# Two position-wise front layers: image-major tokens, rings of three and no hardware loops

## The chip, the core and the metric

The kernel runs on one core of one Trainium2 chip, in one launch. The metric is the device time in microseconds. Before the change it is 6516.77 us, the median of 3 runs (6513.06 to 6520.01). The core has a matrix engine (TensorE, PE in the profile), a vector engine (VectorE, DVE), an activation engine (ScalarE, ACT), a general engine (GpSimd, POOL), and a queue engine (SyncE, SP) that issues most of the DMAs.

## The reference, cut to what matters

The input is 64 images of 32 x 32 positions with 32 channels in float32. Six residual layers follow each other. Only the first two change here:

```
x = x + L0(_gn(x))   # per position (l,h): gelu(x @ W1[l,h] + b1[l,h]) @ W2[l,h] + b2[l,h]
x = x + L1(_gn(x))   # expanded = x @ W_exp.T + b_exp, split in primary and gating (32 + 32)
                     # s = 0.9*s + 0.1*gating along the 32 image rows, s0 = 0
                     # out = (primary * sigmoid(s)) @ W_con.T + b_con
_gn: per image and channel, (v - mean) / sqrt(var + 1e-5) over the 1024 positions
```

After them come a squared-score attention layer, an expert-choice layer, and one block with softmax attention and a router. They read the two layers' output from DRAM as rows `t1` of 32 channels a position, and they make up the larger part of the time.

## The kernel before, in words

`positionwise_layers` does both front layers in one block. Four neighbouring positions of an image row lie with their 32 channels on the 128 partitions, so an image is 256 columns; eight columns are one image row. The tile `xt` holds all 64 images, `[128, 256 columns, 64 images]`: the image is innermost. One chunk is one image row of all images, 8 x 64 = 512 elements a partition; there are 32 chunks a layer (`ROWS`). All engines walk the chunks in hardware loops of two chunks a turn (`pairs`), with two buffers of everything.

- `statistics(n)`, L197 to L219: 64 `bn_stats` of VectorE (L199), one an image, each reading 256 elements that lie 64 words apart. Two small matmuls with `share` (L387) average over the four partition groups, and GpSimd takes the power of minus one half (L168). It runs once ahead of each layer.
- Layer 0. VectorE subtracts the mean (L234), scales (L236), adds the first bias (L244), adds the second bias (L250), and adds to `xt` (L254). TensorE multiplies with the weights of each position, `products` at L397: 8 columns x 4 groups of 32 partitions, each a 32x32 float32 product over 64 images that the trace shows as two matmuls with a weight load each, so 64 matmuls for the first product and 64 for the second. ScalarE does one GELU a chunk (L343). SyncE loads a chunk's two weight tiles (L135, L136) into one of two buffers, once the second product of the chunk two before it is done (`out_made`).
- Layer 1. Three matmuls 128x512 a chunk (L431 main, L432 gate, L436 contraction), each two in the trace. ScalarE scales the gate product by 0.1 (L357), VectorE does the running average `0.9*ema + drive` (L281), ScalarE takes the sigmoid (L362), VectorE gates (L288) and adds to `xt` (L293).
- Rows out. For each image and half, GpSimd copies 128 columns into `staged` (L173), TensorE transposes them (L459), VectorE copies them out of PSUM (L319) and SyncE stores an image (L142).

The order within an engine is the order of its program; semaphores link the engines. The next layer's block begins when all engines have come to the end of this one.

Of the kernel before, what the change touches and what calls it, by code (L numbers as in the profile page):

```python
# [6 lines left out]
F32 = mybir.dt.float32  # L7
BF16 = mybir.dt.bfloat16
ACT = mybir.ActivationFunctionType
# [14 lines left out]
def pairs(eng, lo, hi, body):  # L24

    turns = (hi - lo) // 2
    with eng.Fori(0, turns) as k:
        for u in range(2):
            body(2 * k + (lo + u), (lo + u) % 2)
    if (hi - lo) % 2:  # L30
        body(hi - 1, (hi - 1) % 2)


def positionwise_layers(nc, t):
# [3 lines left out]
    with ExitStack() as ctx:  # L38
        def sb(name, shape, dt=F32):
            return ctx.enter_context(nc.sbuf_tensor(name, shape, dt))  # L40

        def ps(name, shape, dt=F32):
            return ctx.enter_context(nc.psum_tensor(name, shape, dt))

        def sem(name):
            return ctx.enter_context(nc.semaphore(name))

        xt = sb("xt", [P, NI, B])
# [11 lines left out]
        w1 = sb("w1", [P, 2, NC, C])  # L60
        w2 = sb("w2", [P, 2, NC, C])
        xn = sb("xn", [P, 2, CH])
        xc = sb("xc", [P, 2, CH])
        pre = sb("pre", [P, 2, CH])
        hid = sb("hid", [P, 2, CH])
        res = sb("res", [P, 2, CH])
# [5 lines left out]
        b_gate10 = sb("b_gate10", [P, 1])  # L72
        b_con = sb("b_con", [P, 1])
        drive = sb("drive", [P, 2, CH])
        ema = sb("ema", [P, 2, CH])
        gate = sb("gate", [P, 2, CH])
        gated = sb("gated", [P, 2, CH])
        staged = sb("staged", [P, 2, P])
        rows = sb("rows", [P, 2, 2, P])

        p_hid = [ps(f"p_hid{u}", [P, CH]) for u in range(2)]
        p_out = [ps(f"p_out{u}", [P, CH]) for u in range(2)]
        p_gate = [ps(f"p_gate{u}", [P, CH]) for u in range(2)]
        p_rows = [ps(f"p_rows{u}", [P, CH]) for u in range(2)]
        p_stat = p_gate[0]
        p_main, p_con = p_hid, p_out

        loaded = sem("loaded")
        small_loaded = sem("small_loaded")
        zeroed = sem("zeroed")  # L90
        consts = sem("consts")
        w_in = [sem(f"w_in{u}") for u in range(2)]
        chain = sem("chain")
        moment_ready = sem("moment_ready")
        group_made = sem("group_made")
        var_ready = sem("var_ready")
        rstd_ready = sem("rstd_ready")
        centred0 = sem("centred0")
        centred1 = sem("centred1")
        xn_ready = sem("xn_ready")  # L100
        hid_made = sem("hid_made")
        begun = sem("begun")
        pre_ready = sem("pre_ready")
        gelu_ready = sem("gelu_ready")
        out_made = sem("out_made")
        fin_done = sem("fin_done")
        yn_ready = sem("yn_ready")
        split_made = sem("split_made")
        b10_ready = sem("b10_ready")
        drive_ready = sem("drive_ready")  # L110
        ema_ready = sem("ema_ready")
        gate_ready = sem("gate_ready")
        gated_ready = sem("gated_ready")
        con_made = sem("con_made")
        t_ready = sem("t_ready")
        staged_ready = sem("staged_ready")
        turned = sem("turned")
        rows_ready = sem("rows_ready")
        stored = [sem(f"stored{u}") for u in range(2)]
        block = ctx.enter_context(nc.Block())  # L120


        @block.sync
        def _(sp):
            sp.dma_start(xt[:, :, :], t["x"]).then_inc(loaded, 16)
# [2462 lines left out]
```

## Time and profile before

| | us |
|---|---|
| median of 3 runs | 6516.77 |
| profiled execution | 6516.68 |
| its span | 6514.9 |
| loading, to the first statistic | 24.6 |
| statistics and power, layer 0 | 45.9 |
| chunks of layer 0 | 203.3 |
| statistics and power, layer 1 | 46.2 |
| chunks of layer 1 | 219.3 |
| rows out, to the next block's first instruction | 84.7 |
| all that follows | some 5890 |

The stages are stretches of the profiled execution's span, cut at the first subtraction and the last residual of each layer. The four engines' busy time in a stretch can be read beside its length, with the mean clock that TensorE was granted (1.00 is 2.4 GHz, 0.50 is 1.2 GHz) and the share in which the DMA engines were busy. An instruction's busy time is longer than the distance from its start to that of the next, since successive instructions overlap a little. In the timeline the bracket behind an instruction gives its engine's idle time ahead of it, and who ended it. SPq is SyncE's queue.

### The profile page before, as it was taken

Reading aid. Unit: us, or ns where it says so; the run is one execution under the profiler, and the core shown is the slowest. Engines: PE = TensorE matmul, PEld = TensorE weight load, DVE = VectorE, ACT = ScalarE, POOL = GpSimd, SP = SyncE. Lnnn points to the kernel's source line nnn. Section 1 sums busy time; section 2 is a strip of 40 time slices with the busy share of each in tenths; the row PEclk is TensorE's granted clock in tenths of the full one; section 3 lists DMA queues with packets and bytes.
Section 4 is the critical chain, followed back from the end, with each engine's and each line's share of the span. In section 5 each row is a group of like instructions: output and inputs, shape, how many; then the busy total and the mean of one; then the engine's idle time right before and its main releaser. Section 6 shows DMA issues by size and latency. Waiting matters only on the chain.

```text
span 6514.9 us, 148212 instructions
## 1 busy us (share of the span) xinstructions
PE 5454.5 (84%) x43064; PEld 2228.8 (34%) x43064; DVE 5003.2 (77%) x9451; ACT 4806.4 (74%) x8154; POOL 3181.9 (49%) x3788
## 2 busy tenths in 40 slices
PE   3364799999999999955699999998999999989997
PEld 3322344444444444444222222222222222222222
DVE  5543577676766767663899989999999999989995
ACT  0010699898989989921588888888888888888887
POOL 0003577777777777762244444444444444444443
PEclk8575899999999999967799999999999999999999
DMA  2001000000000000023000000000000000000000
GB/s 78 28 0 54 12 10 10 10 10 10 10 10 10 10 10 10 8 56 108 7 9 10 11 9 9 9 9 9 9 10 10 9 9 9 9 9 9 10 9 5
DMA packets 400159, 104.17 MB, mean 16 GB/s; under 512 B 349010, under 2 KB 399139, under 8 KB 399267
## 3 DMA queue, kind: packets, MB, share of 16 engines
q1 hardware_dynamic: 398243, 94.72, 6.7%
q8 instruction: 383, 6.28, 0.4%
q14 instruction: 381, 3.12, 0.2%
q10 hardware_dynamic: 1152, 0.05, 0.0%
HBM read 61.17 MB, written 33.56 MB: 15 GB/s over the span
## 4 chain that ended last, share of the span: by engine, by line
PE 23%; DVE 15%; issue 8%; ACT 3%; POOL 3%; DVEq 1%; DMA 0%; SPq 0%; ACTq 0%; POOLq 0%
DVE d_peaks L2378 12%; PE d_p_o L2206 7%; PE d_p_s L2193 5%; PE d_p_k L2222 4%; ACT d_wt L2089 2%; PE d_p_s L2295 2%; POOL d_rstd L2001 2%; PE d_p_s L2179 1%; PE d_p_s L2253 1%; PE d_p_s L2244 1%; DVE d_total L2388 1%; POOL d_xl L2005 1%; ACT d_answers L2085 1%; DVE d_rank L2470 1%; DVEq L2373 1%
## 5 line engine op out<-in xcount | busy, mean ns | idle before, releaser
L2378 DVE TENSOR_REDUCE d_peaks<-d_p_k 128x1 f32<-128x512 f32 x4096 | 2610.1, 684 | 242.6 <-PE d_p_k L2222 221.1
L2089 ACT ACTIVATE d_wt<-d_p_s 128x512 f32<-128x512 f32 x4096 | 2198.3, 614 | 413.2 <-PE d_p_s L2193 412.4
L853 ACT ACTIVATE b_wt<-b_sq 128x1024 f32<-128x1024 f32 (+3 forms) x1536 | 1240.1, 845 | 12.3 <-issue 12.3
L2206 PE MATMUL d_p_o<-d_wt,d_v_pad 128*32 128x512 f32 x8192 | 1096.6, 607 | 2.3 <-ACT d_o_sb L2094 1.6
L2222 PE MATMUL d_p_k<-d_kT,d_qT 64*128 64x512 bf16 x4096 | 800.4, 385 | 207.9 <-DVE d_peaks L2378 187.1
L762 POOL TENSOR_TENSOR b_sq<-b_sq 128x1024 f32<-128x1024 f32 (+1 forms) x512 | 850.2, 1682 | 233.8 <-DVE b_sq L1077 233.8
L842 ACT ACTIVATE b_sq<-b_p_s 128x1024 f32<-128x1024 f32 (+2 forms) x1024 | 776.3, 758 | 183.1 <-PE b_p_s L913 175.0
L2193 PE MATMUL d_p_s<-d_qT,d_kT 64*128 64x512 bf16 x4096 | 801.5, 387 | 58.1 <-ACT d_wt L2089 40.4
L1077 DVE TENSOR_TENSOR b_sq<-b_p_s,b_tri 128x1024 f32<-128x1024 f32 (+1 forms) x512 | 551.4, 1088 | 278.6 <-PE b_p_s L913 219.4
L2044 POOL TENSOR_TENSOR d_answers<-d_answers,d_mix 128x2048 f32<-128x2048 f32 x64 | 233.1, 3642 | 949.3 <-DVE d_mix L2479 949.3
L926 PE MATMUL b_p_o<-b_wt,b_v_pad 128*32 128x512 f32 (+2 forms) x6144 | 671.9, 510 | 1.8 <-ACT b_wt L853 1.0
L913 PE MATMUL b_p_s<-b_qT,b_kT 64*128 64x512 bf16 (+3 forms) x3072 | 501.6, 338 | 148.7 <-DVE b_sq L1077 120.0
L2193 PEld LDWEIGHTS d_p_s<-d_qT,d_kT 64*128 64x128 bf16 x4096 | 199.0, 93 | 1138.2 <-ACT d_wt L2089 802.1
L1994 POOL TENSOR_TENSOR d_square<-d_centred 128x256 f32<-128x256 f32 x128 | 78.5, 613 | 770.3 <-DVE d_centred L2391 770.3
L913 PEld LDWEIGHTS b_p_s<-b_qT,b_kT 64*128 64x128 bf16 x3072 | 137.2, 93 | 752.8 <-issue 255.0
L2222 PEld LDWEIGHTS d_p_k<-d_kT,d_qT 64*128 64x128 bf16 x4096 | 205.5, 93 | 545.4 <-DVE d_peaks L2378 487.7
L768 POOL TENSOR_SCALAR_AFFINE_SELECT b_sq<-b_sq 128x256 f32<-128x256 f32 x512 | 284.9, 559 | 209.6 <-ACT b_sq L842 185.6
L979 PE MATMUL b_p_m<-b_qkv,b_rel 128*128 128x224 f32 (+7 forms) x1920 | 326.3, 312 | 0.0
L979 PEld LDWEIGHTS b_p_m<-b_qkv,b_rel 128*128 128x128 f32 x1920 | 276.9, 190 | 37.8 <-issue 25.9
L2046 POOL TENSOR_TENSOR d_answers<-d_answers 128x1024 f32<-128x1024 f32 (+2 forms) x192 | 279.8, 1457 | 15.1
L2085 ACT ACTIVATE d_qT<-d_p_s 128x1024 bf16<-128x1024 bf16 x256 | 267.1, 1044 | 20.7 <-PE d_p_s L2263 17.0
L2206 PEld LDWEIGHTS d_p_o<-d_wt,d_v_pad 128*32 128x32 f32 x8192 | 161.4, 108 | 282.6 <-issue 278.1
(293 smaller groups left out, 7744.9 us busy)
## 6 DMA issues: line engine op xcount, KB each, us to landing
c_slots<-t SPq DMA_DIRECT2D x128, 128.0 KB, 2.5
w<-in_L_conv_W SPq DMA_DIRECT2D x64, 128.0 KB, 2.1
t<-rows SPq DMA_DIRECT2D x64, 128.0 KB, 1.8
b_x_in<-t SPq DMA_DIRECT2D x64, 128.0 KB, 2.7
t<-b_result SPq DMA_DIRECT2D x64, 128.0 KB, 2.2
t<-c_slots SPq DMA_DIRECT2D x64, 128.0 KB, 1.8
d_x_in<-t SPq DMA_DIRECT2D x64, 128.0 KB, 2.8
d_x_keep<-t SPq DMA_DIRECT2D x64, 128.0 KB, 2.8
```

What stands on the lines that cost most here:

```text
L762: pool.tensor_tensor(at, at, at, ALU.mult).then_inc(pool_squared, 1)
L842: act.activation(sq[:, n % SQ_RING, :, 0:m], p_s[n % 2][:, :, 0:m], ACT.Square).then_inc(act_squared, 1)
L853: act.activation(wt[:, n % RING, :, 0:m], sq[:, n % SQ_RING, :, 0:m], ACT.Silu, scale=1.0 / D).then_inc(weighed, 1)
L913: pe.matmul(p_s[n % 2][:, r, 0:m], kT[rows, u, g, kb * P:(kb + 1) * P], qT[rows, u, g, q0:q0 + m], start=True, stop=True).then_inc(scored, 1)
L926: ins = pe.matmul(p_o[qc][32 * h:32 * h + 32, q0 - qc * HALF:q0 - qc * HALF + m], v_pad[:, place, kb, h, :], wt[:, (2 * a + h // 2) % RING ...
L979: ins = pe.matmul(at[:, n0 * C:(n0 + count) * C], rel[:, x0:x0 + P], v[:, m0:m0 + count, :].rearrange("p j c -> p (j c)"), start=(d == 0), ...
L1077: dve.tensor_tensor(sq[:, n % SQ_RING, :, 0:m], p_s[n % 2][:, :, 0:m], tri[:, 0:m].rearrange("p (r m) -> p r m", r=1).broadcast_to([P, 2, m]),
L2089: act.activation(wt[:, n % RING, :], tile(n)[:, :], ACT.Exp, scale=SCALE).then_inc(s_used, 1)
L2193: pe.matmul(seat(n + r)[:, :], kT[rows, win.slot("own"), h // 2, kb * P:(kb + 1) * P], qT[rows, win.slot("own"), h // 2, qc * HALF:(qc + 1 ...
L2206: ins = pe.matmul(p_o[32 * h:32 * h + 32, :], v_pad[:, slot, kb, h, :], wt[:, (H * a + h) % RING, :], start=(kb == 0), stop=(kb == J - 1), ...
L2222: pe.matmul(free_bank((m, r))[:, :], qT[rows, slot, g, j * P:(j + 1) * P], kT[rows, slot, g, half * HALF:(half + 1) * HALF], start=True, s ...
L2378: dve.tensor_reduce(peaks[:, m, r:r + 1], bank((m, r))[:, :], X, ALU.max).then_inc(k_used, 1)
```

## The change

`xt` becomes `[128, 64 images, 256 columns]`, and the input is laid out the same way in DRAM. It is loaded in four parts of 16 images with a semaphore each, and the first statistics wait part by part. The 64 `bn_stats` now read 256 adjacent elements. The hardware loops are gone: all engines' programs are written out over the 32 chunks. Weights have a ring of four, the other tiles and the hidden and main PSUM banks rings of three, `p_out` two; `xc` and `res` have one buffer. The normed chunk `xn` lies `[image, column]`, so the first product's moving operand is `xn[q, ring, :, i]`, 64 elements 8 words apart, while the hidden chunk stays `[column, image]`; the second bias reads `p_out` transposed, 64 words apart, and writes `res` as `[image, column]`. The chunk in `xt` is then 64 runs of 8 words.

In layer 1 the average is taken of the normed rows by VectorE ahead of the gate product, and ScalarE makes sigmoid, factor 0.1 and bias in one instruction out of PSUM (the bias of row k is `b_gate * (1 - 0.9**(k+1))`, from 32 small memsets on GpSimd and one product). The `drives` instruction of ScalarE goes, and the feedback from the gate product into the average with it.

Rows out come in 32 fills of a bank: four transposes straight from `xt`, one copy of 512 elements, one store of 256 KB. The first 16 (the upper image halves) are put into the last 16 of the 36 turns of layer 1's loop, copied by ScalarE; the last 16 follow it, copied in turn by ScalarE and VectorE out of four banks. GpSimd's copies go.

```diff
-        xt = sb("xt", [P, NI, B])
+        W_RING, RING, PARTS = 4, 3, 4
+        FILLS = 2 * B // 4
+        EARLY = FILLS // 2
+        xt = sb("xt", [P, B, NI])
...
+            for k in range(ROWS):
+                u = k % W_RING
+                if k >= W_RING:
+                    sp.wait_ge(out_summed, k - W_RING + 1)
+                sp.dma_start(w1[:, u], ...).then_inc(w_loaded[u], 16)
+                sp.dma_start(w2[:, u], ...).then_inc(w_loaded[u], 16)
...
+                for b in range(B):
+                    if n == 0 and b % (B // PARTS) == 0:
+                        dve.wait_ge(x_loaded[b // (B // PARTS)], 16)
+                    dve.bn_stats(stats[:, b, :], xt[:, b, :]).then_inc(chain, 1)
...
+            for k in range(ROWS + 4):            # VectorE, layer 0
+                if k < ROWS:
+                    if k >= RING:
+                        dve.wait_ge(hid_summed, k - RING + 1)
+                    subtract_mean(0, k)
+                    scale(0, k)
+                h = k - 1                        # pre[h] = p_hid[h] + b1, waits hid_summed h + 1, hid_made h - 2
+                f = k - 4                        # res = p_out[f] (p b i) + b2, waits out_summed f + 1; xt row f += res
...
+            for k in range(ROWS + 2):            # TensorE, layer 0
+                if k < ROWS:
+                    pe.wait_ge(w_loaded[k % W_RING], 32 * (k // W_RING + 1))
+                    pe.wait_ge(xn_made, k + 1)
+                    if k >= 3:
+                        pe.wait_ge(pre_made, k - 2)
+                    products(p_hid[k % 3], w1[:, k % W_RING],
+                             lambda q, i: xn[q, k % RING, :, i]).then_inc(hid_summed, 1)
+                g = k - 2                        # second product of g, waits hid_made g + 1, added g - 1
...
+            for k in range(ROWS + 4):            # VectorE, layer 1: xc, xn, ema of k
+                        dve.scalar_tensor_tensor(out=ema[:, k % RING, :], in0=ema[:, (k - 1) % RING, :], scalar=0.9, in1=now,
+                                                 op0=ALU.mult, op1=ALU.add).then_inc(ema_made, 1)
+                g = k - 2                        # gated[g], waits gate_made g + 1
+                f = k - 4                        # xt row f += p_con[f] + b_con, waits con_summed f + 1
...
+            for k in range(ROWS + 4):            # TensorE, layer 1: main(k), gate(k) of ema(k), con(k - 3)
+                f = k - (ROWS + 4 - EARLY)
+                if f >= 0:
+                    turn_rows(f)
+            for f in range(EARLY, FILLS):
+                turn_rows(f)
...
-        "x": lay(i["x"].reshape(B, NI, R * C).transpose(2, 1, 0)),
+        "x": lay(i["x"].reshape(B, NI, R * C).transpose(2, 0, 1)),
```

## Rows read from the trace of the kernel before

**Rows 1.** The page's first line.

```profile
span 6514.9 us, 148212 instructions
```

**Rows 2.** Stretches: bounds and length; busy us (instructions) by engine; clock, DMA, GB/s.

```profile
0.00:24.60 24.60, 0.00 (x0) 0.00 (x0) 0.02 (x1) 1.28 (x1) 3.42 (x18) 1.00 0.91 365
24.60:70.50 45.90, 1.35 (x4) 1.00 (x4) 33.45 (x73) 0.00 (x0) 10.51 (x1) 1.00 0.03 6
70.50:273.80 203.30, 110.30 (x4096) 104.29 (x4096) 107.66 (x160) 21.43 (x33) 0.06 (x1) 0.63 0.13 39
273.80:320.00 46.20, 1.38 (x4) 1.00 (x4) 33.48 (x74) 0.00 (x0) 10.56 (x1) 0.51 0.00 0
320.00:539.30 219.30, 147.95 (x192) 45.22 (x192) 106.48 (x162) 38.67 (x64) 0.00 (x0) 0.75 0.00 0
539.30:624.00 84.70, 46.12 (x128) 23.25 (x128) 31.43 (x129) 0.00 (x0) 47.07 (x128) 0.50 0.33 99
```

**Rows 3.** Timeline at the start: start us, busy us, engine line op.

```profile
24.58 31.21 DVE L199 BATCH_NORM_STATS2 stats<-xt  x64 [24.58 <-DMA b<-in_L_conv_b]
```

**Rows 4.** DMA issues up to 60 us: count, KB each, median us to landing.

```profile
xt<-in_x SPq DMA_DIRECT2D x1, 22.0
```

**Rows 5.** Timeline of layer 0, one chunk.

```profile
129.48 0.33 SPq L135 DMA_DIRECT2D w<-in_L_conv_W  x1
...
131.59 0.69 DVE L236 TENSOR_TENSOR xn<-xc,rstd 128x512 f32<-128x512 f32 x1
...
132.21 1.93 PE L397 MATMUL p_hid<-xn,w 32*32 32x64 f32 x64 [2.94 <-DMA w<-in_L_conv_W]
...
133.89 1.96 PE L397 MATMUL p_out<-hid,w 32*32 32x64 f32 x64
...
136.05 0.33 SPq L135 DMA_DIRECT2D w<-in_L_conv_W  x1
```

**Rows 6.** Timeline of layer 0, TensorE alone, an earlier chunk.

```profile
99.61 1.41 PE L397 MATMUL p_hid<-xn,w 32*32 32x64 f32 x63 [2.90 <-DMA w<-in_L_conv_W]
100.75 0.31 PE L397 MATMUL p_out<-hid,w 32*32 32x64 f32 x1
```

**Rows 7.** Groups by shape, VectorE: busy us, mean ns.

```profile
L199 DVE BATCH_NORM_STATS2 stats<-xt x128 | 62.4, 571 | 24.8 <-DMA b<-in_L_conv_b 24.6 <-DVE xt L254 0.3
...
L1094 DVE TENSOR_REDUCE b_squares<-b_square 128x8 f32<-128x256 f32 x64 | 26.9, 420 | 8.2 <-POOL b_square L773 0.7
...
L1620 DVE TENSOR_REDUCE c_pooled<-c_mine 128x32 f32<-128x256 f32 x8 | 4.8, 603 | 0.3
```

**Rows 8.** Moving operand 16 words apart: ns min/median/max, first and last start.

```profile
L1542 PE MATMUL c_p_t<-c_pooledT,c_w x32: 283/379/403, 2989.5 to 2994.6; 33*128 33x64 f32 x32
```

**Rows 9.** Timeline of layer 1, one chunk.

```profile
403.70 0.74 DVE L293 SCALAR_TENSOR_TENSOR xt<-p_out,b_con,xt 128x512 f32 x1
...
404.36 0.68 DVE L234 TENSOR_TENSOR xc<-xt,mean 128x512 f32<-128x512 f32 x1
405.07 0.69 DVE L236 TENSOR_TENSOR xn<-xc,rstd 128x512 f32<-128x512 f32 x1
405.68 0.68 DVE L281 SCALAR_TENSOR_TENSOR ema<-ema,drive 128x512 f32<-128x512 f32 x1
...
405.81 1.91 PE L431 MATMUL p_hid<-xn,w_main 128*128 128x512 f32 x2
...
407.56 1.02 PE L432 MATMUL p_gate<-xn,w_gate 128*128 128x512 f32 x2
...
409.86 0.75 DVE L288 SCALAR_TENSOR_TENSOR gated<-p_hid,b_main,gate 128x512 f32<-128x512 f32 x1 [3.49 <-ACT gate L362]
```

**Rows 10.** Timeline, first transposes of the rows out.

```profile
539.82 0.81 PE L459 MATMUL p_rows<-ident,staged 128*128 128x128 f32 x2 [1.30 <-POOL staged L173]
```

**Rows 11.** DMA issues of the rows out.

```profile
t<-rows SPq DMA_DIRECT2D x64, 128.0 KB, 1.8
```

**Rows 12.** Instruction fetches, 5000 to 5100 us: packets, MB, share.

```profile
q8 instruction: 6, 0.10, 0.4%
```

More of the change, by code:

```diff
@@ L21, with mid @@
 J = S // P
[L24 to L31, printed above, removed]
+def mid(ap, n):
+    return ap.rearrange("p (j o) -> p j o", o=1).broadcast_to([ap.shape[0], ap.shape[1], n])
 def positionwise_layers(nc, t):
@@ new lines, in positionwise_layers @@
+        gate = sb("gate", [P, RING, CH])
+        gated = sb("gated", [P, RING, CH])
+        rows = sb("rows", [P, 4, CH])
+        bank = [ctx.enter_context(nc.psum_tensor(f"a_p{k}", [P, CH], F32)) for k in range(8)]
+        p_hid, p_out = bank[0:3], bank[3:5]
+        p_main, p_con, p_gate, p_rows = bank[0:3], bank[3:5], bank[5:7], bank[7]
+        p_stat = bank[6]
+        x_loaded = [sem(f"x_loaded{k}") for k in range(PARTS)]
+        b_loaded, small_loaded, zeroed, consts = sem("b_loaded"), sem("small_loaded"), sem("zeroed"), sem("consts")
@@ new lines, in _ @@
+            to = t["rows1"].rearrange("(b h p) c -> p b h c", b=B, h=2)
+            for f in range(FILLS):
+                half, b = fill_of(f)
+                if copied_by_act(f):
+                    sp.wait_ge(rows_act, act_copies(f))
+                else:
+                    sp.wait_ge(rows_dve, dve_copies(f))
+                sp.dma_start(to[:, b:b + 4, half, :], rows[:, f % 4, :].rearrange("p (b c) -> p b c", c=P)).then_inc(stored[f % 4], 16)
+            for u in range(4):
+                sp.wait_ge(stored[u], 16 * FILLS // 4)
@@ L309, in _ @@
-            pairs(dve, 2, ROWS, body1)
-            dve.wait_ge(ema_ready, ROWS - 1)
-            average(ROWS - 1, 1)
-            gating(ROWS - 1, 1)
-            finish1(ROWS - 2, 0)
-            finish1(ROWS - 1, 1)
-            def copy_rows(b, u):
-                for half in range(2):
-                    dve.wait_ge(turned, 2 * b + half + 1)
-                    dve.tensor_copy(rows[:, u, half, :], p_rows[half][:, 0:P]).then_inc(rows_ready, 1)
-            def copy_next(b, u):
-                dve.wait_ge(stored[u], 8 * (b - u))
-                copy_rows(b, u)
@@ L381, in _ @@
+            for f in range(EARLY, FILLS):
+                if copied_by_act(f):
+                    copy_rows(f)
         @block.tensor
@@ L470 @@
+            for f in range(EARLY, FILLS):
+                turn_rows(f)
 H = 4
```

444 lines of the change are left out of this document (180 added, 264 removed).

## The prediction

> **What bounds the kernel now.** I read the page's first line, then cut the span into stretches by the timeline, then read one chunk of each loop in the timeline, and last the forms of the operations that change. The profiled execution takes 6516.68 us, 1.8 us beyond its span [rows 1], and lies 0.1 us from the median, so the sum is made on 6516.7.
>
> The changed block ends at 624.0 us; nothing behind it is touched. In its loops no engine is full: TensorE is busy 110 of 203 us in layer 0 and 148 of 219 in layer 1, VectorE 108 and 106 [rows 2]. The loops run at the pace of round trips.
>
> Layer 0: SyncE issues a weight load at 129.48, as the second product ends; TensorE's next first product starts at 132.21, the second at 133.89, and the next load is issued at 136.05 [rows 5]. That is a closed ring of 6.57 us: 2.73 of load and 3.84 of products. The normed chunk (start 131.59, 0.69 long) comes at nearly the same moment as the weights. Thirty-two such chunks are the 203.3 us.
>
> Layer 1: the gate product feeds the average, the average the sigmoid, the sigmoid VectorE's gating, which waits 3.49 us for it, idle [rows 9]. The period is 219.3 / 32 = 6.85 us.
>
> Rows out: a GpSimd copy, a transpose, a VectorE copy and a store with two buffers each; DMAs move 99 GB/s at a third of their time [rows 2]. And 24.6 us pass before the first statistic starts, since it waits for the whole input and the biases [rows 3, 4].
>
> **The change part by part.**
>
> *Loading and first statistics.* Before: 24.6 + 31.2 = 55.8 us [rows 3]. The whole input lands 22.0 us after its issue [rows 4]; in four parts that land one after the other, the last is there at about 22.8 us and the first at about 7. `bn_stats` starts every 31.21 / 64 = 488 ns and takes 571 for 256 elements 64 words apart. What adjacent elements give is shown by two reductions over 256: 420 ns contiguous, 603 read 32 words apart [rows 7], so hopping costs 183 ns, 0.71 ns an element. That puts a start every 0.31 us; I take 0.33 (bounds 0.31 and 0.488). Sixteen images then take 5.3 us, as long as a part takes to land, so the statistics end at 22.8 + 5.3, say 28.5: -27.3. Bounds: with no gain from adjacency 7 + 31.2 = 38; if all parts land together, 22.8 + 21 = 44.
>
> *Second statistics.* 64 x (0.488 - 0.33) = -10.1 us; between -11.4 and 0. The small steps and the power behind them, about 14.7 us a layer (45.9 - 31.2 [rows 2, 3]), stay; the mean is now subtracted from the first chunk under the power, which I leave out of the sum (0.7 us twice).
>
> *Layer 0.* With weights four deep, a load is issued two turns of TensorE ahead of its use with one whole turn in between: 2.73 us against 3.6. The wait for them goes. The next limit is VectorE's own work: the same five operations a chunk. Their distances, read in layer 1 where they run back to back, are 0.61 for one that depends on nothing just before it (xn to the average, 405.07 to 405.68), 0.66 behind the fused add, 0.71 for one that waits for its predecessor (404.36 to 405.07) [rows 9]. So xc 0.71, xn 0.61, first bias 0.61, second bias 0.71, residual 0.61: 3.25. The second bias now reads PSUM 64 words apart: 512 x 0.71 = 0.37 us more by the SBUF rows (bounds 0 and twice that). Runs of 8 words I cost at nothing, for between hops they are adjacent; the bound above is a hop's 0.71 ns per run, 0.05 us an operation. Period 3.65.
>
> TensorE under it: 64 matmuls start in 1.68 us, 26.3 ns each, between the two products [rows 5]; at another chunk 63 start in 1.14 us, 18.1 ns each [rows 6]; the mean clock is 0.63 [rows 2]. A chunk is 3.4 us at the slow pace: just below VectorE. The first product's moving operand becomes strided by 8 words. The one strided moving operand in the trace has 32 matmuls in 5.1 us, 165 ns each, with a 128-column weight load in every one [rows 8]; with four partition groups side by side that bounds it at 41 ns; the lower bound is the contiguous 26.3, or 18.1. I take the contiguous value, since the weight load explains the 165.
>
> So 32 x 3.65 = 117, and 2.5 of filling (first product and GELU behind the first chunk; at the end the last residuals of VectorE cover the last product): 119.5 for 203.3, -83.8. What the waits queue: TensorE's wait for the normed chunk k stands ahead of the second product of k - 2, and VectorE's wait for `out_summed` ahead of the next chunk's subtraction, but the product it asks for was issued two turns earlier.
>
> *Layer 1.* VectorE keeps five operations: xc 0.71, xn 0.71 (the average now depends on it), average 0.61, gating 0.67, residual 0.66: 3.36, against an old period of 6.85. Gating runs two turns behind the average and the contraction three, so no answer is awaited in the same turn. ScalarE falls from two operations to one. TensorE has six matmuls; two take 1.75 us from 405.81 to 407.56, 0.87 each, and later one of the pair 0.5 [rows 9]: between 2.6 (all at the full clock, half of 5.25) and 5.25 us a chunk. The busier TensorE is, the more of the time at the full clock I expect (0.75 here, 0.50 where it mostly waits [rows 2]), so I take VectorE as the limit. From the 20th turn a fill is added: four transposes, start to start 0.34 at clock 0.50 [rows 10], 0.7 to 1.4 us. That makes the last twelve turns some 0.2 us longer. At the end four turns carry only contractions and fills, each fill waiting for ScalarE's copy of the fill before it in the single bank, 1.6 us a turn. 32 x 3.36 = 107.5, 2.5, 9: 119 for 219.3, -100.3.
>
> *Rows out.* Sixteen fills remain behind the loop. Each reuses its buffer after four: copy 0.7, issue 0.5, landing 1.8 for half the size [rows 11], say 2.5: 3.9 us for four, and 4.2 MB at the 300 GB/s that 99 at a 0.33 share comes to [rows 2] are 14 us. I take 1.05 us a fill, 17, with 2 for the fills that the loop leaves over, 2.5 for the last landing and 2.5 for the change of block as now: 24 for 84.7, -60.7. GpSimd's 47 us go; they only mattered here.
>
> Sum: 27.3 + 10.1 + 83.8 + 100.3 + 60.7 = 282.2. 6516.7 - 282.2 = 6234.5, so 6235 us.
>
> By the Trainium skill (Advanced Engine Details and Errata, Memory Cachelines) an SBUF access that goes to another 16-byte line each time is penalised, and a non-contiguous pattern in PSUM slows matmuls markedly. That speaks against the strided moving operand and the transposed reading of `p_out`. The two reductions of rows 7 agree for VectorE; for TensorE no run here separates it from the weight load.
>
> **The rivals.**
>
> *A: TensorE is the bound.* For it: a mean clock of 0.63 and 0.75 in these loops now, though they are two thirds full [rows 2], and a margin of 0.25 us in layer 0. Against: its gaps shrink to under 1 us. Strided products at 41 ns make layer 0's chunk 64 x 0.041 + 1.68 = 4.3, plus 21 us in all; a slow clock throughout layer 1 makes 20 turns of 5.25 and 12 of 6.5 plus 14 at the end, 197, plus 78. Whole: 6334; if half of it comes, 6285.
>
> *B: instruction fetch.* Layer 0's TensorE program is now 128 matmuls and 128 weight loads a chunk in a straight line. Later stretches fetch 6 blocks of 16 KB in 100 us, each holding its DMA engine 0.004 x 16 x 100 / 6 = 1.07 us [rows 12]. If the code takes a block a chunk, it needs one every 3.65 us, beside weight loads. If each were awaited in full, with a load's 2.7 us, layer 0 would get 32 x 2.7 = 86 longer: 6321. Against: 1.07 is less than a chunk.
>
> The Trainium skill (Runtime: NRT & Kernel Launch, Instruction fetch mechanics) holds that straight code is fetched a page ahead and its crossing mostly hidden, while a taken branch can break it. By that rule B costs nothing; no row here has TensorE's code in a straight line at this pace.
>
> *C: slower than before.* The strided products lose their overlap across the four groups. There are 32 x 64 = 2048. Each may take (3.65 - 1.68) / 64 = 31 ns for nothing; beyond that the gain of 282 is eaten from 31 + 282 / 2.048 = 169 ns each. At 165 the time is 6509, even; at the full 379 ns of a record [rows 8], not pipelined at all, +713: 6948. Against: nothing but the stride changes, and the matmuls of rows 8 do overlap.
>
> **How the numbers follow.** Forecast 0.65, A 0.20, B 0.10, C 0.05. Within 0.2%, 13 us, this kernel can't be told from unchanged. Forecast, A and B are all faster: 0.95. C splits: 0.04 slower, 0.01 the same. The forecast's own range, from its bounds, is 6205 to 6265 (statistics +16, second bias +12, layer 1 and fills +-15). For 8 in 10 it reaches into A and B: 6200 to 6315.
>
> **What would show it.** First statistic near 7 us, `bn_stats` near 390 ns, the power starting near 33. Layer 0's chunks 3.65 us apart with VectorE hardly idle, its second bias near 1.06 us; no weight wait. Layer 1's near 3.4 with the clock near 1.00. The next block starting near 342 us. It would be wrong if TensorE is full in either loop, if its idle time is put to issue once a chunk, or if the parts land together.

## The result, and the profile after

The changed kernel takes 6222.01 us, the median of 4 runs (6216.34 to 6226.75), against 6516.50 of the kernel before (6513.06 to 6520.01): ratio 0.9548, 95% interval 0.9531 to 0.9564. The forecast was 6235. Its profiled execution is the shortest of the four, 6216.34 us, 300.3 below that of before. The changed block accounts for 291.2 of them: it now ends at 332.8 us, not at 624.0. The other 9 or so lie in the untouched rest, which took 5890.9 us before and 5881.7 here. In the experiments below that rest comes to between 5884 and 5902 us, so I compare kernels by stages of the changed block, and whole times only beyond that spread.

First line of the page, then the stretches of the block (bounds, length, busy us and instructions of TensorE, its weight loads, VectorE, ScalarE and GpSimd, granted clock, DMA share, GB/s); they answer to [rows 1, 2]:

```profile
span 6214.5 us, 145806 instructions
...
0.00:8.27 8.27, 0.00 (x0) 0.00 (x0) 0.00 (x0) 0.00 (x0) 4.46 (x50) 1.00 0.81 312
8.27:45.56 37.29, 1.35 (x4) 1.00 (x4) 24.05 (x74) 1.28 (x1) 10.94 (x1) 1.00 0.53 193
45.56:165.10 119.54, 99.27 (x4096) 92.00 (x4096) 104.22 (x159) 21.45 (x33) 0.00 (x0) 0.97 0.23 66
165.10:200.70 35.60, 1.38 (x4) 1.00 (x4) 24.01 (x75) 0.00 (x0) 10.42 (x1) 0.52 0.00 0
200.70:312.40 111.70, 99.19 (x252) 41.92 (x252) 105.12 (x159) 30.57 (x47) 0.66 (x1) 0.97 0.11 31
312.40:332.80 20.40, 10.30 (x68) 8.81 (x68) 5.53 (x8) 5.76 (x11) 0.01 (x1) 0.86 0.89 244
```

| stage | before | after | gain | forecast |
|---|---|---|---|---|
| load, statistics, power of layer 0 | 70.5 | 45.6 | 24.9 | 27.3 |
| layer 0 | 203.3 | 119.5 | 83.8 | 83.8 |
| statistics and power of layer 1 | 46.2 | 35.6 | 10.6 | 10.1 |
| layer 1 | 219.3 | 111.7 | 107.6 | 100.3 |
| rows out | 84.7 | 20.4 | 64.3 | 60.7 |
| sum | 624.0 | 332.8 | 291.2 | 282.2 |

The row of layer 1 begins at 200.70 us; its first scaling starts at 201.40, so 0.7 us of it belong to the power ahead of it.

VectorE is busy 104 of 120 us and 105 of 112 in the two loops, where it had been busy half the time.

Timeline of the start, VectorE (start us, busy us, and in brackets what it waited for); it answers to [rows 3]. The first line is two parts, for the second had landed when the first was done:

```profile
8.27 10.55 DVE L176 BATCH_NORM_STATS2 a_stats<-a_xt 128x6 f32<-128x256 f32 x32 [8.27 <-DMA a_xt<-in_x]
19.31 5.32 DVE L176 BATCH_NORM_STATS2 a_stats<-a_xt 128x6 f32<-128x256 f32 x16 [0.49 <-DMA a_xt<-in_x]
25.09 5.33 DVE L176 BATCH_NORM_STATS2 a_stats<-a_xt 128x6 f32<-128x256 f32 x16 [0.46 <-DMA a_xt<-in_x]
```

Thirty-two statistics in 10.55 us are one every 0.33, as forecast. The two waits, 0.49 and 0.46, show that the stage goes at the pace of the transfers, with VectorE close behind.

Timeline of layer 0, one chunk:

```profile
90.17 0.68 DVE L202 TENSOR_TENSOR a_xc<-a_xt,a_mean 128x512 f32<-128x512 f32 x1
...
90.95 0.69 DVE L207 TENSOR_TENSOR a_xn<-a_xc,a_rstd 128x512 f32<-128x512 f32 x1
...
91.82 0.69 DVE L223 TENSOR_TENSOR a_pre<-a_p,a_b 128x512 f32<-128x512 f32 x1 [0.17 <-PE a_p L327]
92.42 0.68 DVE L232 TENSOR_TENSOR a_res<-a_p,a_b 128x512 f32<-128x512 f32 x1
...
92.59 0.91 PE L327 MATMUL a_p<-a_hid,a_w 32*32 32x64 f32 x49 [0.62 <-issue]
93.14 0.69 DVE L236 TENSOR_TENSOR a_xt<-a_res,a_xt 128x512 f32<-128x512 f32 x1
...
93.29 2.09 PE L327 MATMUL a_p<-a_xn,a_w 32*32 32x64 f32 x64
...
93.75 0.68 DVE L202 TENSOR_TENSOR a_xc<-a_xt,a_mean 128x512 f32<-128x512 f32 x1
...
95.95 0.91 PE L327 MATMUL a_p<-a_hid,a_w 32*32 32x64 f32 x49 [0.38 <-issue]
```

From one subtraction to the next it is 3.58 us, and 0.17 of that is a wait for TensorE, so VectorE's own work is at most 3.41 here. Over the whole loop the first five scalings come within 8.7 us (45.59 to 54.32), since those turns have no residual yet; the 27 intervals after them are 3.69 us on average (to 153.99). Read the second bias (L232): it starts 0.60 us behind the first bias and lasts 0.68, though it reads PSUM 64 words apart. And read TensorE: its second product is cut in two, with a hole that the profile puts to `issue`, which means that the engine waited for nothing that the profile shows. Twenty microseconds earlier, TensorE alone:

```profile
67.39 0.85 PE L327 MATMUL a_p<-a_hid,a_w 32*32 32x64 f32 x42 [0.15 <-issue]
...
70.97 0.86 PE L327 MATMUL a_p<-a_hid,a_w 32*32 32x64 f32 x43 [0.41 <-issue]
```

Behind the hole stand 42 matmuls, then 43, and at 92.59, six chunks on, 49. The hole comes once a chunk and wanders back about one matmul a chunk. A chunk is 256 matmuls and weight loads, and a few instructions more; so the hole marks a fixed length of code of about 256 instructions. The instruction fetches of 50 to 150 us (packets, MB, share of the 16 engines) and the waits of 45 to 160 us (total, times, longest), nearly all of layer 0:

```profile
q8 instruction: 27, 0.44, 1.9%
```

```profile
PE a_p L327 <- issue: 15.1, 26, 1.1
...
DVE a_pre L223 <- PE a_p L327: 9.6, 19, 1.7
```

Twenty-seven blocks of 16 KB in 100 us: one a chunk. The holes are 15.1 / 26 = 0.6 us on average, and their ends are 3.62 us apart on average (60.39 to 158.08, 27 blocks), the longest 3.94, the shortest 3.31. Of them and of the strided product together VectorE feels 9.6 us, its whole wait for the first product.

Timeline of layer 1, one chunk; it answers to [rows 9]:

```profile
230.89 0.68 DVE L202 TENSOR_TENSOR a_xc<-a_xt,a_mean 128x512 f32<-128x512 f32 x1
...
231.67 0.69 DVE L207 TENSOR_TENSOR a_xn<-a_xc,a_rstd 128x512 f32<-128x512 f32 x1
232.40 0.69 DVE L254 SCALAR_TENSOR_TENSOR a_ema<-a_ema,a_xn 128x512 f32<-128x512 f32 x1
...
233.01 0.74 DVE L261 SCALAR_TENSOR_TENSOR a_gated<-a_p,a_b_main,a_gate 128x512 f32<-128x512 f32 x1
...
233.67 0.74 DVE L266 SCALAR_TENSOR_TENSOR a_xt<-a_p,a_b_con,a_xt 128x512 f32<-128x512 f32 x1
...
234.33 0.68 DVE L202 TENSOR_TENSOR a_xc<-a_xt,a_mean 128x512 f32<-128x512 f32 x1
```

3.44 us a chunk, VectorE without a gap, at a clock of 0.97. DMA issues of 305 to 345 us (count, KB, us to landing), which answer to [rows 11]:

```profile
t<-a_rows SPq DMA_DIRECT2D x22, 256.0 KB, 2.8
```

### The profile page after: what moved, and what is told of

Same layout as the page of the kernel before. It is cut to its first block, busy times and chain, and to the rows that moved or that the text cites. A ratio compares the mean times of both kernels' runs of the same rounds, so it can differ in the third digit from the quotient of the medians.

```text
span 6214.5 us, 145806 instructions
## 1 busy us (share of the span) xinstructions
PE 5346.4 (86%) x43064; PEld 2191.6 (35%) x43064; DVE 4957.7 (80%) x9330; ACT 4801.7 (77%) x8146; POOL 3128.8 (50%) x3692
## 4 chain that ended last, share of the span: by engine, by line
PE 24%; DVE 16%; issue 8%; ACT 3%; POOL 3%; DVEq 1%; DMA 0%; SPq 0%; ACTq 0%; POOLq 0%
DVE d_peaks L2296 12%; PE d_p_o L2124 7%; PE d_p_s L2111 5%; PE d_p_k L2140 5%; ACT d_wt L2007 2%; PE d_p_s L2213 2%; POOL d_rstd L1919 2%; PE d_p_s L2097 1%; PE d_p_s L2171 1%; PE d_p_s L2162 1%; DVE d_total L2306 1%; POOL d_xl L1923 1%; ACT d_answers L2003 1%; DVE d_rank L2388 1%; DVEq L2291 1%
## 5 line engine op out<-in xcount | busy, mean ns | idle before, releaser
L2111 PE MATMUL d_p_s<-d_qT,d_kT 64*128 64x512 bf16 x4096 | 801.4, 387 | 60.7 <-ACT d_wt L2007 40.4
## 6 DMA issues: line engine op xcount, KB each, us to landing
a_xt<-in_x SPq DMA_DIRECT2D x4, 2048.0 KB, 14.7
```

The lines of the kernel that those rows point to most:

```text
L2111: pe.matmul(seat(n + r)[:, :], kT[rows, win.slot("own"), h // 2, kb * P:(kb + 1) * P], qT[rows, win.slot("own"), h // 2, qc * HALF:(qc + 1 ...
```

## The experiments

A stage is read from its first scaling to the end of its last residual. For layer 0 of the changed kernel that is 119.5 us, with a hole of 0.6 us on average a chunk and a first product of 64 matmuls in 1.86 us (93.29 to 95.15); for layer 1 it is 111.0 (201.40 to 312.38).

Experiments 1 to 10 are one execution each. Experiments 8, 9 and 10 leave layer 0 as it is, and it takes 120.6, 121.2 and 121.4 us there, so a difference under 2 us in layer 0 shows nothing. Layer 1 takes 110.9 to 111.4 us wherever an experiment leaves its program alone or only deepens its rings.

**1. First product reads adjacent words.**

```diff
-                             lambda q, i: xn[q, k % RING, :, i])
+                             lambda q, i: xn[q, k % RING, :, :].rearrange("p b i -> p (b i)")[:, i * B:(i + 1) * B])
```

> Changed kernel with one edit: in layer 0 the first product's moving operand is 64 adjacent words of the normed chunk instead of 64 words that lie 8 apart. It multiplies other elements than the reference asks for (an image's columns stand where a column's images should); counts and shapes are unchanged. Theory T (TensorE sets layer 0's chunk of 3.5 us: 64 strided matmuls in 1.86 us, a hole of some 0.6 us, 64 contiguous in 0.95): the strided product falls from 1.86 to some 0.95 us, TensorE needs 2.5 us a chunk, VectorE's five operations (3.3 us) become the bound, and the stretch from the first scaling to the last residual falls from 119.5 to about 110 us. Rival V (VectorE's own work sets the chunk, the stride is hidden under it): first product again near 1.86 or hidden, stretch unchanged at 119 to 120 us. Whole time by T about 6210, by V about 6220.

Measured: 6227.33 us, layer 0 117.5. TensorE alone:

```profile
94.63 0.91 PE L327 MATMUL a_p<-a_hid,a_w 32*32 32x64 f32 x49 [1.52 <-issue]
...
98.14 0.91 PE L327 MATMUL a_p<-a_hid,a_w 32*32 32x64 f32 x50 [1.52 <-issue]
```

The 64 matmuls of the first product start within 0.9 us (91.83 to 92.72), where they took 1.86: the stride costs (1.86 - 0.9) / 64 = 15 ns a matmul. But the hole grew from 0.6 to 1.52 us, and the chunk is still 3.51 (94.63 to 98.14). Over the loop the hole ends are 3.62 us apart (54.69 to 156.03, 28 blocks), exactly as with the strided product. What TensorE saves, the hole takes. Neither theory had this: a block of code comes no sooner for holding 1 us less work.

**2. TensorE's layer 0 as a hardware loop over four chunks.**

```diff
+            for k in range(4):
+                turn0(k, k, 32)
+            with pe.Fori(1, ROWS // 4) as t4:
+                for u in range(4):
+                    turn0(4 * t4 + u, u, 32 * t4 + 32)
```

`turn0` is the old body; the rings are four deep and the first product has four banks, so that a chunk's place in them is fixed in the loop.

> Changed kernel with TensorE's layer 0 put back into a hardware loop: four chunks ahead of it, then seven turns of four chunks, rings of four for xn, pre, hid and four PSUM banks for the hidden chunk; the order of the work is the same. Question: what the hole of 0.2 to 0.8 us is that TensorE shows once a chunk in the second product, put down to issue, and that moves back by one matmul a chunk. Theory F (instruction fetch: a chunk is 256 instructions, 16 KB, one fetched block): with a resident loop body the fetches in the stretch fall from 30 to a few, the hole vanishes, TensorE needs 2.85 us and the stretch falls from 119.5 to about 110 us (VectorE's 3.3 a chunk). Rival Q (the hole is a wait for weights or for the queue): fetches fall, the hole stays, stretch 119 to 120. Rival R (a loop of 64 KB doesn't stay resident): fetches stay at one a chunk and nothing moves, or the branch adds a stall of 1 to 3 us each of seven turns, stretch 120 to 140.

Measured: 6222.42 us, layer 0 111.3; the block ends at 325.4 us. TensorE alone, and the fetches of 50 to 150 us:

```profile
91.30 2.06 PE L328 MATMUL a_p<-a_xn,a_w 32*32 32x64 f32 x64 [0.35 <-DVE a_xn L208]
93.17 1.10 PE L328 MATMUL a_p<-a_hid,a_w 32*32 32x64 f32 x64
94.97 2.06 PE L328 MATMUL a_p<-a_xn,a_w 32*32 32x64 f32 x64 [0.70 <-DVE a_xn L208]
```

```profile
q8 instruction: 6, 0.10, 0.4%
```

The hole is gone with the fetches (6 for 27), the second product runs in one piece, and TensorE now waits for VectorE. All six lie ahead of 72 us, when the loop's body is fetched for its first turn; from 72.5 to 150 us there is none, and from 83 us on the scalings are 3.32 to 3.33 us apart, all but one. So the hole is instruction fetch, and it costs the change 8.2 us, up to 10 against the other executions of the same layer 0. The deeper rings that the loop needs came with it; in layer 1, which has them too, they give nothing (111.4 us against 111.0). The whole time doesn't show the gain: the rest took 5895 us in this execution and 5882 in the changed kernel's.

**3. Both.**

The edits of 1 and 2 together.

> Both edits at once: TensorE's layer 0 in the loop of four chunks, and the first product on 64 adjacent words (other elements than the reference asks for). If TensorE is the bound by both (T and F), TensorE needs 1.9 us a chunk, but either edit alone has already handed the bound to VectorE, so the stretch is about 110 us, as in each alone, and VectorE is idle under 2 us in it. If neither matters (V) it is 119 to 120. If the loop costs a stall a turn (R), it is longer than with adjacent words alone by that stall.

Measured: 6217.00 us, layer 0 108.4, block end 321.9. The stride costs 2.9 us more (111.3 against 108.4), 2.4 of them in the first eleven intervals, most of them from the time in which the code is still fetched; later the scalings are 3.32 to 3.33 us apart in both, all but one. TensorE is busy 70.7 us instead of 96.3. Of the 108.4 that remain VectorE is busy 102.0. Where nothing holds it up, its five operations take 3.32 us from one scaling to the next (91.50 to 94.82). A caution for readers of such rows: TensorE's idle time ahead of the second product, 20.2 us in 23 pieces, is put to issue here too, though no block is fetched between 71 and 150 us. The word alone does not show a fetch; the count of blocks and the place that wanders do.

**4. Weight loads left out.** Is the fetch slow because it shares the DMA engines with the weights?

```diff
+                if k < W_RING:
                     sp.dma_start(w1[:, u], ...)
                     sp.dma_start(w2[:, u], ...)
-                    pe.wait_ge(w_loaded[k % W_RING], 32 * (k // W_RING + 1))
+                    pe.wait_ge(w_loaded[k % W_RING], 32)
```

The first product reads adjacent words, as in 1.

> Changed kernel with adjacent words for the first product (other elements than asked for) and no weight loads beyond the first four chunks, whose weights are used again (so the products of the other 28 chunks are not the reference's). Question: why TensorE's hole grew from 0.6 to 1.5 us a chunk when its products got 0.95 us shorter, so that a block of 256 instructions still took 3.5 us. Theory C (the fetch of a block waits behind the weight loads on its DMA engine): without them the hole shrinks to under 0.5 us, the chunk falls to VectorE's 3.35, the stretch from 117.6 to about 109 us. Theory L (the fetch has its own pace, 3.4 to 3.5 us a block, whatever else the DMA engines do): hole 1.5 us again, stretch 116 to 118.

Measured: 6224.07 us, layer 0 120.9.

```profile
92.32 0.91 PE L326 MATMUL a_p<-a_hid,a_w 32*32 32x64 f32 x49 [1.52 <-issue]
...
95.82 0.91 PE L326 MATMUL a_p<-a_hid,a_w 32*32 32x64 f32 x49 [1.52 <-issue]
```

The same 1.52 us hole, the same 3.50 us between these two, with 56 transfers of 128 KB fewer. Over the loop the hole ends are 3.74 us apart (54.29 to 158.99, 28 blocks), not less than in experiment 1, and layer 0 is 3.4 us longer, where Theory L had 116 to 118. So the weight loads are not what makes a fetch slow.

With the weights gone the fetches stand alone in the DMA engines' throughput. Here are 92 to 100 us, each column 0.2 us; a column of 82 GB/s is one block of 16 KB (the 41 ahead of the first is another queue's):

```profile
GB/s 0 0 0 0 0 41 82 0 0 0 0 0 0 0 0 0 0 0 0 0 0 0 0 0 82 0 0 0 0 0 0 0 0 0 0 0 0 0 0 0
```

TensorE enters a block at 92.32; the next block's packet starts in the column of 93.2, about 1 us later, and TensorE goes on at 95.82. The packets in the trace of the changed kernel show this step by step for 23 blocks: the packet starts 1.0 to 1.2 us after TensorE has entered the block before, takes 0.9 to 1.4, and TensorE goes on 1.3 to 1.5 us after its end. Together that is 3.3 to 3.9 us, and the longer packets make the longer blocks. So the pace looks like a round trip, with the next block asked for only once the block before it is entered. No run changes when it is asked for, so this is a reading of the trace and not shown by an experiment. Here a packet takes 1.12 us on average and in experiment 1 1.03, which over 28 blocks is some 2.5 of the 3.4 us.

**5. GpSimd subtracts the mean** (from the third chunk on; layer 0's normed chunk becomes column by column, which makes the moving operand adjacent too). It asks what VectorE's five operations hold back.

```diff
+                for k in range(2, ROWS):
+                    pool.wait_ge(xn_made, ROWS * n + k - 1)
+                    pool.tensor_tensor(view(n, xc[:, k % 2, :]), chunk_of_x(n, k), spread(n, mean[:, :]),
+                                       ALU.subtract).then_inc(centred, 1)
```

> A version meant to be faster: from the third chunk of each layer GpSimd subtracts the mean, two chunks ahead, into one of two buffers; in layer 0 the centred and normed chunks are laid column-major, so that TensorE reads 64 adjacent words. VectorE keeps four operations a chunk. If VectorE's count sets the pace: layer 0 goes from 3.6 to about 2.7 us a chunk (VectorE 2.6, TensorE 0.95 + 0.95 + a hole of 0.6), the stretch from 119.5 to about 90; layer 1 from 3.44 to about 2.95 (TensorE's six matmuls 2.6 and a fill 0.5), the stretch from 111.7 to about 97; whole time about 6175. Rival: GpSimd's subtraction (0.6 us for 256 elements elsewhere in this trace, so 1.2, or 2 with a strided read) slows VectorE's operations that run beside it, since both read the same memory: then VectorE's operations grow beyond 0.70 us and the gain is under half.

Measured: 6205.65 us. Layer 1 falls from 111.0 to 93.7 us, 3 below the expected 97: 2.65 us a chunk, and 3.02 once the fills join, which VectorE no longer hides. Layer 0 stays at 118.1: it should have fallen to 90, and the hole is there again, with VectorE now waiting behind it:

```profile
95.00 0.91 PE L353 MATMUL a_p<-a_hid,a_w 32*32 32x64 f32 x49 [1.52 <-issue]
...
98.50 0.91 PE L353 MATMUL a_p<-a_hid,a_w 32*32 32x64 f32 x50 [1.52 <-issue]
```

**6. The same with the loop of 2.** If 3.5 us a block is the bound, layer 0 must fall once the code stays in place.

> GpSimd's subtraction from the third chunk on, column-major normed chunks in layer 0, and TensorE's layer 0 in the loop of four chunks, so that no block is fetched. If instruction fetch held layer 0 at 3.5 us with four VectorE operations a chunk (118.1 us), it now runs at VectorE's 2.65 us a chunk: stretch about 90 us, whole time about 6180. Rival: GpSimd's strided subtraction (its chunk took over 2 us) or the weights, whose loads are issued only two turns ahead (2.7 us of landing against 2.65 of turn), take its place: chunks of 3.0 to 3.3 us, stretch 98 to 108.

Measured: 6184.62 us, layer 0 97.1, layer 1 93.8. Timeline of layer 0, GpSimd and VectorE:

```profile
95.22 0.68 DVE L229 TENSOR_TENSOR a_xn<-a_xc,a_rstd 128x512 f32<-128x512 f32 x1
...
95.98 1.52 POOL L178 TENSOR_TENSOR a_xc<-a_xt,a_mean 128x512 f32<-128x512 f32 x1 [1.23 <-DVE a_xn L229]
...
97.13 0.92 DVE L261 TENSOR_TENSOR a_xt<-a_res,a_xt 128x512 f32<-128x512 f32 x1
...
97.97 0.68 DVE L229 TENSOR_TENSOR a_xn<-a_xc,a_rstd 128x512 f32<-128x512 f32 x1
```

A chunk is 2.75 us (95.22 to 97.97), below the 3.5 and more that every straight-line version had. The expected 90 was missed mostly by the residual add: 0.92 us beside GpSimd's transposed read of `xt`, 0.23 more a chunk. In experiment 5 the same add takes 0.69 where GpSimd is idle (at 91.15 us) and 0.92 where it runs (at 55.85).

**7. Weights three deep.** Is the fourth ring place what took the load wait away?

```diff
-        W_RING, RING, PARTS = 4, 3, 4
+        W_RING, RING, PARTS = 3, 3, 4
```

> Changed kernel with a weight ring of three instead of four: chunk k's weights may be loaded only once the second product of k - 3 is done, and that is TensorE's last work ahead of the first product of k. So the load's round trip (issue, 2.1 to 2.7 us to landing) stands between any two turns again, as in the kernel before, while everything else of the change stays. If the exposed round trip was what held the old loop at 6.57 us: chunks of 2.8 + 2.8 to 3.5 = some 6 us, the stretch of layer 0 from 119.5 back to about 190 us, whole time about 6295. Rival (the deeper VectorE and TensorE pipeline made the gain, the weights were a bystander): chunks of 3.6 to 4.5 us, stretch 120 to 145.

Measured: 6308.29 us, layer 0 201.3: of the 83.8 us gained 2 are left. Waits of layer 0, and TensorE in it:

```profile
PE a_p L327 <- DMA a_w<-in_L_conv_W: 78.8, 29, 3.2
```

```profile
96.21 2.08 PE L327 MATMUL a_p<-a_xn,a_w 32*32 32x64 f32 x64 [2.66 <-DMA a_w<-in_L_conv_W]
```

The load goes out at 93.61, behind the second product that freed its place, and TensorE stands for it: the closed ring of [rows 5] again. The mean clock is 0.64 (0.97 with four), so part of the loss is TensorE at 1.2 GHz for part of the time. There is no hole: at 6.3 us a chunk the fetch has time.

**8. Gating in the same turn.** Is the distance of two turns what halved layer 1?

```diff
-                g = k - 2
+                g = k
                 if 0 <= g < ROWS:
                     dve.wait_ge(gate_made, g + 1)
```

> Changed kernel with one edit in layer 1: VectorE gates chunk k in turn k instead of turn k + 2, so it waits in the same turn for average, gate product and sigmoid. From this kernel's rows: the gate product starts 0.98 us after the average does, its two matmuls are 1.06 us later done, the sigmoid takes 0.69: VectorE is idle about 1.9 us a chunk behind the average. If the depth in turns made layer 1's gain, the chunk goes from 3.44 to about 5.4 us and the stretch from 111.7 to about 172 us, whole time about 6280; the clock of TensorE falls below 0.97. Rival (most of the gain comes from the operation that ScalarE lost and from the average's feedback that is gone, and the depth adds little): chunk under 4.2, stretch under 137.

Measured: 6351.46 us, layer 1 238.3 (111.0 with two turns), 7.4 us a chunk, worse than the kernel before. Waits of 202 to 440 us:

```profile
DVE a_gated L261 <- PE a_p L385: 111.9, 29, 4.9
...
DVE a_gated L261 <- ACT a_gate L305: 12.0, 3, 4.3
```

Right direction, wrong size: I had expected 172 for the round trip to ScalarE. Most of the wait is put down to the contraction (L385): TensorE has it in its queue behind the gate product, at the clock that the waiting brings, 0.74, and gating waits on the contraction's semaphore as well, since the ring of three frees its place by that. So the distance is needed for the gain. What the lost `drives` operation and the feedback that went with it are worth by themselves, no run shows.

**9. The input in one transfer.**

```diff
-        W_RING, RING, PARTS = 4, 3, 4
+        W_RING, RING, PARTS = 4, 3, 1
```

> Changed kernel with the input loaded in one part instead of four. The first statistic then waits for all 8.4 MB, at about 24.6 us as in the kernel before, and 64 of them at 0.33 us follow: the power starts at 24.6 + 21.1 + 4.2 = 50 us instead of 34.6, and the block ends some 15 us later; whole time about 6236. Rival (the input's landing is no bound, the gain came from the adjacent words alone): power starts before 40 us.

Measured: 6240.74 us. VectorE's start:

```profile
22.89 21.01 DVE L176 BATCH_NORM_STATS2 a_stats<-a_xt 128x6 f32<-128x256 f32 x64 [22.89 <-DMA a_xt<-in_x]
```

All statistics follow the transfer, and the first scaling comes at 59.1 us instead of 45.6: 13.5 us for the four parts. The rest of that stage's 24.9, 11.4, is the adjacent reading (21.01 against 31.21 for 64, [rows 3]: 10.2) and the start of the statistics at 22.89 instead of 24.58, since they no longer wait for the biases (1.7); the steps and the power behind them took 0.4 longer. The mean subtracted under the power is no part of it: the subtraction stood behind this stage before.

**10. All row fills behind layer 1.**

```diff
-                f = k - (ROWS + 4 - EARLY)
-                if f >= 0:
-                    turn_rows(f)
-            for f in range(EARLY, FILLS):
+            for f in range(FILLS):
                 turn_rows(f)
```

> Changed kernel with all 32 fills of rows out behind layer 1's loop, in four banks, copied in turn by ScalarE and VectorE. Theory D (the stores are bound by the DMA engines at some 285 GB/s): 8.4 MB take 29 us and with the first fill and the last landing the stretch from the last residual to the next block is about 35 us instead of 20.4, while layer 1 is shorter by the 2 to 3 us that its last four turns wait for fills: the block ends 12 to 14 us later, whole time about 6234. Rival S (the last 16 fills are bound by the ring of four buffers and its landing, 1.2 us each): 32 x 1.2 = 38 and more, block 18 to 22 us later.

Measured: 6250.67 us. Layer 1 takes 110.2 us instead of 111.0, so the sixteen fills inside cost it 0.8 us; the block ends at 346.5, 13.7 later. Throughput of 310 to 350 us, each column 1 us:

```profile
GB/s 0 0 0 0 0 211 285 291 281 287 277 282 280 288 293 287 283 285 293 269 288 244 106 278 285 293 289 283 285 286 286 284 280 284 293 160 0 8 0 0
```

The stores run at some 285 GB/s, but for one dip in the middle: Theory D. What stands behind the loop is bounded by DMA, not by transposes or copies.

**11. A faster version of both kernels.** Experiment 6 with ScalarE's square root and VectorE's reciprocal in place of GpSimd's power.

```diff
-                pool.tensor_tensor(rstd[:, :], var[:, :], minus_half[:, :], ALU.pow).then_inc(rstd_made, 1)
+            act.activation(root[:, :], var[:, :], ACT.Sqrt).then_inc(rooted, 1)
...
+                dve.wait_ge(rooted, n + 1)
+                dve.reciprocal(rstd[:, :], root[:, :]).then_inc(rstd_made, 1)
```

> A version meant to beat both: GpSimd's subtraction and the loop of four chunks, and the power of minus one half on GpSimd (10.9 us before each layer, with every other engine waiting) replaced by a square root on ScalarE (its table loaded ahead) and a reciprocal of 64 elements on VectorE. From rows of the kernel before, a reciprocal takes 203 ns for 8 elements and 252 for 16, so about 0.6 us for 64; the square root of 64 elements about 0.3. Each layer begins its chunks some 9.5 us earlier; the two tables that then stand ahead of the first GELU and the first sigmoid (1.28 us each) are hidden behind the first products in part. Whole time 6184.6 - 18 = 6167 us; if the table loads come onto the path 6170. Rival: GpSimd's first subtraction comes only after the reciprocal either way, and the chunks' start is then held by it or by the weights: under 12 us of gain.

Measured: 6158.01 us, median of 5 (6146.32 to 6163.56), against 6516.01 of before: ratio 0.9448, 0.9435 to 0.9461, which doesn't meet the change's 0.9531 to 0.9564. Timeline:

```profile
34.22 0.26 ACT L317 ACTIVATE a_root<-a_var 128x64 f32<-128x64 f32 x1 [19.55 <-DVE a_var L216]
...
35.04 0.53 DVE L219 RECIPROCAL a_rstd<-a_root 128x64 f32<-128x64 f32 x1
35.50 0.91 DVE L225 TENSOR_TENSOR a_xc<-a_xt,a_mean 128x512 f32<-128x512 f32 x1
36.34 1.27 DVE L234 TENSOR_TENSOR a_xn<-a_xc,a_rstd 128x512 f32<-128x512 f32 x2
```

The first scaling starts at 36.3 us where it started at 45.6, layer 0 is 96.5 and layer 1 93.4, and the block ends at 273.6, 20.1 before that of experiment 6 (293.7), where 18 were expected. The line at 35.50 is VectorE's subtraction with `xt` read transposed, out of SBUF in steps of 256 words, with GpSimd idle: 0.91 us, against 0.68 for the same subtraction with runs of 8 words in layer 1 (at 158.99).

## Why the prediction was right, and where a step failed

**The mechanism.** Both loops ran at the pace of round trips, and the change took the round trips out: that was the reading of [rows 5, 9], and experiments 7 and 8 each bring one back (layer 0 119.5 to 201.3, layer 1 111.0 to 238.3; in layer 1 it is not the same one as before, since gating there waits for a contraction too). Next in line in layer 1 were VectorE's five operations, as said: 3.44 us a chunk without a gap, and 2.65 with one operation less (experiment 5). In layer 0 they were not. With the same operation less, layer 0 stays at 118.1 us; it falls only once the code stays in place (experiments 2 and 6). The fetch of TensorE's code sets that loop's pace. The prediction had named the sign of it, idle time put to issue once a chunk, as one that would show it wrong, and here it came.

**The number.** 6235 against 6222.01: the block gained 9.0 us more than forecast, by terms of layer 1 and rows out. The untouched rest moved by as much from one execution to the next.

**Layer 0: the exact 83.8 is luck.** The forecast pace was 3.65 us, from VectorE's own work; the measured one, from the fifth scaling on, is 3.69, from the fetch. Several terms were off, and they cancel.
- The second bias: "512 x 0.71 = 0.37 us more by the SBUF rows". This step failed. L232 takes 0.68 us and starts 0.60 behind the one before it: PSUM read in hops costs VectorE nothing here. [Rows 7] are about SBUF, and there an operation of the same form does pay for hops (0.91 against 0.68, experiment 11). I had the bound of nothing and took the row of the other memory.
- Scaling starts 0.78 us behind subtraction, not 0.71. The other distances were right, so VectorE's own chunk is 3.32 (experiment 3), not 3.65 (3.25 and 0.37 are 3.62, which I had rounded up).
- The strided moving operand: "I take the contiguous value". It costs 29 ns a matmul against 14 at the full clock (experiment 1), near 1 us a chunk. Alone it would fit under VectorE.
- Instruction fetch, rival B: the hole is 0.6 us a chunk on average, not 2.7, but a block comes only every 3.62 us, which is more than VectorE's 3.32. This is the other step that failed: "1.07 is less than a chunk" counts the packet alone, and 2.5 us more stand around it (experiment 4). VectorE waits for the first product 19 times, 9.6 us in all.
- The start: the first four intervals take 8.7 us, where four chunks of 3.65 had made 14.6. I had left out that these turns have no residual. So the 32 scalings are 3.50 us apart on average (45.59 to 153.99).
- The end: behind the last scaling come four residuals of 1.5 us each, a wait of 1.7 us and the rest of a chunk, 11.1 us together, where one chunk and 2.5 of filling had made 6.2. The short start paid for it.

**The rules weighed.** The Trainium skill (Advanced Engine Details and Errata, Memory Cachelines) has SBUF accesses to ever another line penalised, which speaks against the strided moving operand: the trace agrees, 29 against 14 ns. Of its rule on PSUM the transposed reading by VectorE shows nothing; of matmuls into PSUM no run here has a strided case. The Trainium skill's rule that a page boundary is mostly hidden in straight code (Runtime: NRT & Kernel Launch, Instruction fetch mechanics) does not hold at this pace: 0.6 us of 3.6 stand open, and 1.5 where TensorE has less work. Nor does the fetch stall that the same section ascribes to a taken branch show here: the loop of 1024 matmuls and weight loads fetches 6 blocks where the straight code fetches 27, and none after its first turn.

**Rivals.** A, TensorE as the bound, came true in one part, its stride, and not in the other: the mean clock rose to 0.97 in both loops, nearly all at the upper level, from 0.63 and 0.75. B was real and small in cost, and it is what bounds layer 0. C was out: 29 ns stand beside the 31 that each matmul might take for nothing. With less on VectorE, B would have been the forecast; experiment 5 is that case.

**Layer 1** was forecast 7.3 us too long, 8.0 read from its first scaling. The pace was 3.44, 0.08 above the forecast, by the same 0.78. But the first four turns lack operations (scalings at 201.40, 203.25, 205.37, 208.26), so the 32 scalings are 3.31 apart on average, and nothing was left of the 2.5 of filling. The end took 8.5 us from the last scaling, where one more chunk and the 9 had made 12.4. The fills, forecast at 0.2 us a turn, cost 0.8 us in all (experiment 10).

**Loading** came 2.4 us short: the first part landed at 8.27, not at 7, and the last at 25.09, not at 22.8. By 25.09 us the DMA engines had moved 8.9 MB (354 GB/s), half a megabyte more than the input: weights and biases, issued beside it, at that rate some 1.4 us. In experiment 9 the whole input was there at 22.89 us, after 8.5 MB at 373 GB/s. So they explain a good half of it by this estimate; why four parts moved at the lower rate is open. **Rows out** came out 3.6 better: sixteen fills of 256 KB at 285 GB/s are 14.7 us, where I had 17 for them and 2 for those left over; copies and transposes run beside the stores.

## What to carry to other kernels

When a loop runs at the pace of a round trip, put each consumer as many turns behind its producer as it takes for the answer to be there, and give a ring the place that lets a load go out a whole turn ahead: one weight place fewer cost 82 of 84 us. Before unrolling small matmuls, divide the code of a turn by its time; under some 3.6 us for 256 instructions of TensorE the fetch is the bound, and a hardware loop of some chunks lifts it. When a stage comes out to the tenth, look at what set its pace before calling the forecast right: layer 0 matched with another engine's bound. A price for a strided read is taken from a row of the same engine and the same memory, or both ends stay open.

## What the runs showed of the hardware that I had not expected

- TensorE's straight code comes at one 16 KB block (256 instructions) per 3.3 to 4.3 us, 3.62 on average, with 3 us of work in it as with 2, and no faster without weight loads beside it (3.74). A block occupies its DMA engine for only 0.019 x 16 x 100 / 27 = 1.1 us. The rest is 1.1 us ahead of the packet and 1.4 behind it (experiment 4).
- Square root and reciprocal of 128x64 take 0.26 and 0.53 us; GpSimd's power takes 10.9.
- VectorE, 128x512: reading PSUM in steps of 64 words takes 0.68 us, no more than adjacent words; reading SBUF in steps of 256 words takes 0.91.
- GpSimd reading `xt` transposed slows VectorE's add on it from 0.69 to 0.92 us.
- TensorE's mean clock: 0.97 where its gaps are under 1 us, 1.00 in layer 0 of experiment 1 with gaps of 1.5, 0.64 with gaps of 2.7 us (experiment 7), 0.74 with 3.0 (experiment 8).
